# A planner that orders a four-block network by the longest path to the end, and fills TensorE's planned gaps with constant matmuls

## The reference, cut to what matters

```
x = x + attn_a(layernorm(x))     # 16 heads of 8; q,k,v; 11 scales of shifts
x = x + ffn(layernorm(x))        # 8 experts, top-1: gelu(x W1[e] + b1[e]) W2[e] + b2[e]
x = x + attn_b(layernorm(x))     # a recurrence over the positions, then a layernorm
x = x + ffn(layernorm(x))        # the same experts again

attn_a:  gains = softmax(q . W_qscale + prior)           # over the 11 scales
         out  += gains[j] * D4[tau] * sum(q * k_shifted) * v_shifted      # shifts of 2^j * tau
         return (out * sigmoid(x @ W_gate.T + b_gate)) @ W_out.T + b_out
attn_b:  h = tanh(h @ A.T + x_t @ B.T);  y = h @ C.T     # 512 steps, one behind the other
```

## Time and profile before

| | us |
|---|---|
| median of 3 runs | 1426.97 |
| lowest, highest | 1420.13, 1428.18 |
| the profiled execution (its span, first to last instruction) | 1436.4 |
| PE busy in it | 1170.8 (82%) |
| DVE busy in it | 796.3 (55%) |
| ACT, POOL busy in it | 651.3 (45%), 788.6 (55%) |
| mean granted clock of PE | 0.858 |

### The profile page before, as it was taken

The page is one execution under the profiler, slowest core; times in us unless marked ns, Lnnn a source line. Parts: engine busy times, 40 slices in busy tenths (PEclk is TensorE's granted clock), DMA queues, the critical chain, the costliest instruction groups (busy, mean ns, idle before and its releaser), DMA issues. The chain is left out here.

```text
span 1436.4 us, 32831 instructions
## 1 busy us (share of the span) xinstructions
PE 1170.8 (82%) x9942; PEld 881.1 (61%) x9942; DVE 796.3 (55%) x1723; ACT 651.3 (45%) x2050; POOL 788.6 (55%) x1274
## 2 busy tenths in 40 slices
PE   3877886888888899789988899887899998995580
PEld 2644554566565666466655666676787777785570
DVE  4878788889966777576788647542122301240110
ACT  2233332465544664455554436363564344562250
POOL 2645458563776748862748844876315642324504
PEclk9989987999988998889999759788995567998895
DMA  4700001221221212111112221233332324444542
GB/s 126 213 1 0 1 1 47 61 65 58 86 66 44 64 44 70 51 51 38 44 46 86 60 63 46 77 97 105 108 104 77 98 83 123 118 132 121 146 116 60
DMA packets 117638, 107.58 MB, mean 75 GB/s; under 512 B 15540, under 2 KB 88541, under 8 KB 117469
## 3 DMA queue, kind: packets, MB, share of 16 engines
q1 hardware_dynamic: 106704, 88.01, 21.5%
q0 software_dynamic: 8192, 16.79, 3.9%
q10 hardware_dynamic: 2573, 0.69, 0.2%
HBM read 76.73 MB, written 28.70 MB: 73 GB/s over the span
## 5 line engine op out<-in xcount | busy, mean ns | idle before, releaser
L799 POOL TENSOR_TENSOR acc<-acc,term 128x512 f32<-128x512 f32 x219 | 281.5, 1286 | 71.9 <-DVE term L1341 54.8
L1160 PE MATMUL bank<-w,hT 128*128 x1088 | 217.5, 324 | 22.1 <-ACT hT L985 13.9
L1341 DVE TENSOR_TENSOR term<-bank,V 128x512 f32<-128x512 f32 x251 | 168.0, 684 | 67.2 <-PE bank L1110 44.0
L1005 ACT ACTIVATE hid<-bank 128x16 f32<-128x16 f32 x512 | 93.0, 182 | 243.6 <-PE bank L1187 203.0
L985 ACT ACTIVATE hT<-bank,b1T 128x128 f32<-128x128 f32 x544 | 165.2, 370 | 79.2 <-PE bank L1147 65.2
L839 POOL DMA_INDIRECT back<-sorted_y,slot_i x128 | 125.1, 978 | 135.8 <-DMA back<-sorted_y,slot_i 44.2
L1160 PEld LDWEIGHTS bank<-w,hT 128*128 128x128 f32 x1088 | 173.9, 221 | 41.1 <-issue 35.6
L1187 PEld LDWEIGHTS bank<-hid,abcT 128*32 128x32 f32 x4096 | 88.6, 116 | 162.2 <-ACT hid L1005 83.2
L1312 DVE SCALAR_TENSOR_TENSOR made<-bank,qkvb,K 128x512 f32<-128x512 f32 x251 | 176.2, 742 | 17.8 <-PE bank L1083 7.2
L1187 PE MATMUL bank<-hid,abcT 128*32 128x16 f32 x4096 | 138.6, 201 | 38.3 <-ACT hid L1005 37.1
L1147 PE MATMUL bank<-xTb,w1b 128*128 128x128 f32 x864 | 166.8, 321 | 3.2 <-ACT xTb L973 3.0
(11 more groups left out here) (177 smaller groups left out, 2153.4 us busy)
## 6 DMA issues: line engine op xcount, KB each, us to landing
w1b<-in_W SPq DMA_DIRECT2D x130, 256.0 KB
K<-in_W SPq DMA_DIRECT2D x54, 256.0 KB
xsb<-sorted_x SPq DMA_DIRECT2D x184, 64.0 KB
sorted_y<-ysb SPq DMA_DIRECT2D x136, 64.0 KB
X<-in_x SPq DMA_DIRECT2D x64, 64.0 KB
out_x<-X SPq DMA_DIRECT2D x64, 64.0 KB
sorted_x<-K SPq DMA_DIRECT2D x14, 256.0 KB, 3.6
sorted_y<-made SPq DMA_DIRECT2D x48, 64.0 KB
```

Source lines behind the costliest of these rows:

```text
L799: nc.gpsimd.tensor_tensor(acc[:], acc[:] if k > 1 else term[0][:], term[k % NTERM][:], ALU.add).then_inc(S["terms_added"], 1)
L1005: nc.scalar.activation(hid[n % 2][:, cs], bank[6 + n % 2][:, cs], ACT.Tanh).then_inc(S["h_ready"], 1)
L1160: last = nc.tensor.matmul(bank[SLOT_BANK[place(n)]][:, 0:D], tile(hT[place(n)], c), w2[:, ds(second[n] + c * D, D)], start=(c == 0), stop= ...
L1341: V_.tensor_tensor(term[k % NTERM][:], bank[2 + k % 2][:], V[:, at:at + CW], ALU.mult).then_inc(S["terms_ready"], 1)
```

## The change

The computation stays as it is: the same pieces with the same operands. What changes is the table of numbers and the rule from which the order comes, and how the gaps are filled.

- **Lengths.** Each piece now has two lengths, `pace` (until the engine can begin the next piece) and `took` (until its result is there), and each pair of engines has a hop. An activation-table switch, a turn of PE to the recurrence's column groups, and the transfers' landings are added.
- **Rule.** `to_go` is the longest path from a piece to the end of the program. Of the pieces of an engine that can begin now or within 0.15 us, the planner takes the one with the longest `to_go`, with a penalty of 50 us for each us by which it would begin late. The better rank of `step` and `state` is gone.
- **Fillers.** A planned gap of 0.11 us or more may be filled, with a matmul for each 0.11 us of it, as long as the planned columns in a stretch of length `SPAN_US` up to the end of the next piece are under `TARGET`; of longer gaps, what lies ahead of that stretch is filled fully. Bank 0 may be used too: such a group waits for the piece that closed the bank's turn before it.
- **A few more dependences** are told to the planner (norms in order, `xT` after `vproj`), which were kept by queues before.

The core of the diff (the tables of lengths shortened):

```diff
-PE_PACE = 0.93
-IDLE_US, FILL_US, FILL_SHARE, FREE_US = 0.5, 0.15, 0.65, 1.0
+PACE = dict(
...
+    rows=(0.42, 0.60), rxb=(0.93, 1.06), ry=(0.92, 1.06), step=(0.18, 0.25), turn=(0.12, 0.27), xT=(0.45, 0.60),
...
+HOP_OF = {("state", "step"): 0.05, ("step", "state"): 0.07, ("turned", "hidden"): 0.05, ("hidden", "gelu"): 0.13,
+          ("gelu", "result"): 0.13, ("result", "yadd"): 0.14, ("yadd", "turn"): 0.15, ("slots", "scatter"): 0.29}
...
+TABLE_US, TURN_US, LOOK_US, DAWDLE = 1.283, 0.11, 0.15, 50.0
...
-                choice = (at, todo[key][2], ready, key)
-                if pick is None or choice[0] < pick[0] - 1e-9 or (abs(choice[0] - pick[0]) < 1e-9 and choice[1:3] < pick[1:3]):
-                    pick = choice
...
+        to_go[key] = max((hop(todo, key, y) + to_go[y] for y in followers[key]), default=todo[key].took)
...
+            if r <= now + LOOK_US:
+                choice = (DAWDLE * max(0.0, r - now) - to_go[key], key)
+                if best is None or choice < best[0]:
+                    best = choice, max(r, now)
...
+SPAN_US, TARGET, FILL_US, FILL_COLS, FREE_US = 3.4133, 6000, 0.11, 256, 0.3
...
-        if best and end and BEGIN[key] - best[0] > IDLE_US:
-            out[key] = int((BEGIN[key] - best[0]) * FILL_SHARE / FILL_US), best[1], best[2]
...
+        lack = TARGET - sum(c for _, c in recent) - columns_of(*key)
+        most = int((at - since) / FILL_US)
+        if end and lack > 0 and most > 0:
+            late = sum(since + FILL_US * j > stop - SPAN_US for j in range(most))
+            times = most - late + min(late, -(-lack // FILL_COLS))
+            out[key] = times, b, x
...
-                    if reader:
+                    if reader and b == 0:
+                        pe.wait_ge(S["bank0_taken"], filled)
+                    elif reader:
```

More of the change, by code:

```diff
@@ L192, in past, with pieces, piece @@
+def pieces():
+    todo = {}
+    def piece(engine, what, n, k, after, bank0=None):
+        todo[what, n, k] = Piece(engine, *cost(what, n, k), [x for x in after if x is not None], bank0)
     def past(what, n, k=0):
         return (what, n, k) if n >= 0 else None
-    URGENT, USUAL = 0.0, 1.0
     for i in range(CHUNKS):
@@ L282, in timeline @@
-        piece("DVE", "resid", i, 0, 0.7, USUAL, [("out", i, 0)], bank0=0)
+                piece("POOL", "add", i, j, [("term", i, j), ("add", i, j - 1) if j > 1 else None, past("out", before)])
+        piece("PE", "gatep", i, 0, [("xcopy", i, 0), past("gate", before)], bank0=1)
+        piece("ACT", "tanh", i, 0, [("gatep", i, 0)], bank0=0)
+        piece("DVE", "gate", i, 0, [("add", i, n - 1), ("tanh", i, 0)])
+        piece("PE", "out", i, 0, [("gate", i, 0)], bank0=1)
+        piece("DVE", "resid", i, 0, [("out", i, 0)], bank0=0)
@@ L376, in timeline @@
-    engines = ["SP", "POOL", "ACT", "PE", "DVE"]
-    left = {key: len(x[3]) for key, x in todo.items()}
+            piece("PE", "step", c, k, [("state", c, k - 1) if k else past("state", c - 1, CT - 1), ("rxb", c, 0) if k == 0 else None])
+            piece("ACT", "state", c, k, [("step", c, k), past("ry", c - 2) if k == 0 else None])
+        piece("PE", "ry", c, 0, [("state", c, CT - 1)])
+        piece("DVE", "rres", c, 0, [("ry", c, 0)])
+        piece("DVE", "rstats2", c, 0, [("rres", c, 0), past("rmom2", c - 2)])
@@ L378, in timeline @@
+def timeline():
+    todo = pieces()
     followers = {key: [] for key in todo}
     for key, x in todo.items():
-        for y in x[3]:
+        for y in x.after:
+            assert y in todo, (key, y)
             followers[y].append(key)
-    can, free = {e: {} for e in engines}, {e: 0.0 for e in engines}
+    to_go, left = {}, {key: len(x) for key, x in followers.items()}
+    ends = [key for key, m in left.items() if m == 0]
+    while ends:
+        key = ends.pop()
+        to_go[key] = max((hop(todo, key, y) + to_go[y] for y in followers[key]), default=todo[key].took)
+        for y in todo[key].after:
+            left[y] -= 1
+            if left[y] == 0:
+                ends.append(y)
+    engines = ["PE", "ACT", "DVE", "POOL", "SP"]
+    left = {key: len(x.after) for key, x in todo.items()}
+    can, free = {e: {} for e in engines}, dict(BEGINS)
@@ L440, in fillings @@
             if best is None or since < best[0]:
[L441 to L445 removed]
+                best = since, b, x
+        recent = [x for x in recent if x[0] > stop - SPAN_US]
+        since, b, x = best
+        lack = TARGET - sum(c for _, c in recent) - columns_of(*key)
```

323 lines of the change are left out of this document (173 added, 150 removed).

## The result

| | before | after |
|---|---|---|
| median of the runs taken together, us | 1425.43 (1420.13 to 1428.18) | 1358.78 (1353.72 to 1364.32) |
| ratio | | 0.956, interval 0.949 to 0.963 |
| span of the profiled execution, us | 1436.4 | 1351.7 |
| mean granted clock | 0.858 | 0.973 |
| PE busy, us | 1170.8 | 1224.3 |

The change is faster by 67 us. The forecast was 1253 us, faster by 174 than the 1427 us on record then. The measured time lies at the edge of the range (1185 to 1360), and the gain is little more than a third of the forecast one.

The account below looks back on a forecast made before the run. TensorE's throughput and queue order were taken as the bound, except in the head. 863 us to attention's end plus 399 us behind it made 1262 us; 9 off for the median gave 1253 us, range 1185 to 1360.

Parts of the forecast that it names:

- The order's gain: Whole kernel: attention's pieces first and steps later pack VectorE denser, and steps begun promptly close TensorE's gaps; 88 us without clock.
- part 1: Up to attention's end: VectorE's 690 us of work packed at 80% density, ending at 863 us instead of 943.
- part 2: From attention's end to the end: slots and steps, slow clock, tail and half the waits sum to 399 us, against 457.
- the prediction's own mark: Attention's last `resid` near 863 us; above 905 us the order gained nothing up to there.
- Three quarters of the half-clock time: Share of the lower clock that the new fillers remove: 38 us gained in the middle, 48 us behind attention.
- the 0.93 asked for: Sign over the span: a granted clock of 0.93 or more, with no stretch of tens of us at 0.5.
- Rival (c): Whole kernel: filling small gaps does not raise the clock, so its 86 us go; 1339 us, chance 0.04.
- I cost them at nothing: From `rT` of chunk 0 on: 906 more fillers fit existing TensorE gaps and cost nothing; upper bound 107 us.
- The clock's term: Gain from less time at the lower clock: 38 us in the middle plus 48 us behind attention, 86 us.
- Rival (b): Behind the head: half of the fillers' 107 us falls on the path; 1307 us, with all 1360; chance 0.15.
- the 200 named: Sign for fillers in the way: states' wait for steps stays at 200 us or more while the clock is high.
- Rival (d): Recurrence put off too far, a step taking 1.31 us: 1478 or 1469 us, slower than before; chance 0.06.

Follow-up runs that it names:

- e2: The changed kernel without its 582 fillers ahead of steps, 1517 fillers remaining: 1334.9 us, ratio 0.939 to the kernel before.
- f1: The changed kernel with only the 1075 fillers in the head, ahead of the recurrence's first set-up: 1329.8 us, ratio 0.931 to the kernel before.
- e3: The changed kernel's order with the filler rule of the kernel before, 730 fillers: 1318.2 us, ratio 0.927 to the kernel before.
- e1: The changed kernel with none of its 2099 fillers: 1347.4 us, ratio 0.946 to the kernel before.
- i1: The kernel before, unaltered, run again for a second profile, which had one late release of TensorE: 1432.3 us, ratio 1.004.
- f4: The changed kernel with 0.2 us of each gap kept back and 0.12 us counted per filler, 1315 fillers: 1318.6 us, ratio 0.923 to the kernel before.
- f3: The changed kernel with all 2099 fillers 64 columns wide instead of 256: 1464.0 us, ratio 1.024 to the kernel before.

## Why the prediction was wrong, point by point

- **What bounds the kernel: right.** TensorE's throughput and queue. Where it gets less to do ahead of steps, the kernel gets faster (e2, f1, e3).
- **The order's gain: right in size, by luck.** The order's share of the forecast, without the clock, was 174 - 86 = 88 us: 80 - 38 = 42 up to attention's end and 94 - 48 = 46 behind it. At the clock of before, e1 measured 83 in all, but it has attention's end at 930 us and 414 us behind it, where before has 925 and 492 in i1, and 943 and 493 in the profile with stops. So part 1 gained between nothing and 13 us and part 2 79: one is too high and the other too low by about the same. Part 1, attention's end at 863 us from 80% density on VectorE, did not happen: 925 us in after, 903 in e3, 900 in f4, the best. The density was 72% in after, where TensorE is busy for 853 of 925 us; that steps taken later only make room there which slots and fillers fill is my reading, and no run shows it. By the prediction's own mark (above 905 us the order gained nothing there) this part fell. Part 2, 399 us in the forecast, came to 414 in e1, 413 in e3 and 427 in after.
- **The clock answers to fillers: right, and more than I took.** Three quarters of the half-clock time were to go; the mean went from 0.858 to 0.973, above the 0.93 asked for. Rival (c), that it doesn't answer, is excluded by e1 and after: 0.859 and 0.973 with the same order. In f3 TensorE was busy for 261 of the 267 us from 33 to 300 us, its longest idle time there was 1.4 us, and the granted clock was 0.66. By the rule of the Trainium skill, "TensorE: Matmul & The Clock Gate", Part 1, fillers in gaps of a fraction of a us would have changed nothing. The rows of f3 disagree with that rule: there the clock was low with no idle time over 1.4 us. The pair of e1 and f1 alone would not settle it, since e1 also has idle times of 3 to 6 us in its head.
- **The step that failed: "I cost them at nothing".** The gaps of the plan were not there at run time. The prediction bounded the price by 107 us behind the head at 0.118 each, and chose the end at zero. Worked out above, the fillers there cost 0.07 to 0.11 each, 70 us for 825, and the timeline shows 0.12 for one ahead of a step, where e2's cycle had 0.11 us free and the filler needs more. The clock's term was 86 us of gain; clock and fillers together came out at 11 us of loss against none (e1 to after) and 41 against the old rule's 730 (e3 to after). Without the fillers ahead of steps 24 of these come back. Of the 106 us between 1253 and 1359 the fillers' price makes 70, by the estimates above. Another 28 are gain of the clock that didn't come (86 forecast, 38 behind the head and 20 in it found) and 5 the order's. The reason is in the rule: it fills each gap to the brim with 0.11 us a piece, in a chain where the state and the step follow each other within 0.1 us. A filler that begins just before the state ends delays the step by what is left of it, and in a serial recurrence the next step can't make up for it: states waited 197 us for their steps with the fillers and 160 without (e1).
- **Where the clock gains: wrong.** The prediction gave the head's half clock no price, because VectorE is the bound there. Fillers in the head gained 18 to 22 us: the first state came 20 us earlier. Behind the head the clock's gain of some 38 us was more than eaten up by the fillers' 70.
- **Rival (b), fillers in the way, was right**, nearly with its sign as written: the clock high and the states' wait at 197 us, just under the 200 named. Its place too, the steps. Its range, 1307 to 1360, holds 1359. It had 0.15.
- **Rival (d), slower than before**, by the recurrence put off, did not happen without the stops: last state at 1200 us. With them the changed kernel is slower than before, by 4.8%; the pace of a step is what decides, as (d) said, but by a cause that I didn't look for, though the profile of before, made with stops, held it: 107 late releases and 28 us of states waiting for "remote".

## What to carry to other kernels

A filler is cheap only where something else is the bound, as VectorE is in this head, and f3 shows that fillers at the lower clock can undo that. In the queue of an engine that feeds a serial chain a filler can cost its full 0.12 us. So plan gaps with a reserve of at least the filler's length or leave them open ahead of the chain's link. A granted clock near one is not a gain by itself: e3 at 0.930 beats the changed kernel at 0.973 by 41 us. And before two versions are compared that ran on different occasions, run one of them again beside the other: here the same kernel gave 1359 and 1505 us, and only the repeat showed that 0.21 us for a filler is a wrong price.

## What the hardware showed that I had not expected

- In some groups of executions TensorE's releases come 0.6 to 7 us late (four of some 1300 later still, up to 10.4) while GpSimd issues indirect DMAs, 107 times in before and 168 in the changed kernel; in others once or twice. The kernel before takes 1425 to 1436 us with or without, the changed order 146 us more with them.
- The width of a constant matmul sets what it does for the clock, and its cost only in some places: nine in a row took 1.09 us with 64 columns and 1.23 with 256, but ahead of a step one added 0.04 us with 64 and 0.12 with 256. 64 columns left the head at five to seven tenths of the clock, 256 held it at nine or more.
- TensorE was busy for 261 of 267 us (f3, 33 to 300 us) at a mean granted clock of 0.66, with no idle time over 1.4 us.
- With 582 of 2099 fillers taken out, just those ahead of steps, the clock went only from 0.973 to 0.945.
